# Output projection by output block, gates behind each block, router by input channel block, and the query projected second

## The reference, cut to what matters

```python
# attention of layer 0, per batch: y is what the recurrence gave
q, k, v = x @ Wq.T * K ** -0.5, x @ Wk.T, x @ Wv.T
g = log_sigmoid(x @ Wg.T)
...
o = layernorm(y, gamma, beta) @ Wo.T
x = x + o
# condition of the expert layer, ratio = num / den of the two-sided sum
h = sigmoid(x) * (num / den) * (0.8 + 0.2 * tf)
# router and shared expert
scores = sigmoid(h @ gate_weight.T)          # 16 experts, top 6 of them are picked
shared = down(silu(gate(h)) * up(h))         # 704 inner channels, of every token
```

## Time and profile before

| | us |
|---|---|
| three executions | 3680.26, 3672.75, 3676.23; median 3676.23 |
| the profiled execution, own time | 3678.08 |
| its span, first to last instruction | 3676.3 |
| TensorE clock granted, mean over the span | 0.948 of full |
| busy: PE / DVE / ACT / POOL | 3287.4 / 2605.3 / 1227.3 / 511.8 |

### The profile page before, as it was taken

The page is one execution under the profiler, slowest core; times in us unless marked ns, Lnnn a source line. Parts: engine busy times, 40 slices in busy tenths (PEclk is TensorE's granted clock), DMA queues, the critical chain, the costliest instruction groups (busy, mean ns, idle before and its releaser), DMA issues.

```text
span 3676.3 us, 37190 instructions
## 1 busy us (share of the span) xinstructions
PE 3287.4 (89%) x12621; PEld 2021.7 (55%) x12621; DVE 2605.3 (71%) x3645; ACT 1227.3 (33%) x2145; POOL 511.8 (14%) x404
## 2 busy tenths in 40 slices
PE   1979979979988999999999949899989999999999
PEld 1654654644645767777777714644464446444644
DVE  7888988889875677888888435664667456755664
ACT  2333343332422545434343223312341134113410
POOL 1003003003003111111111021120121012100200
PEclk9989989989999999999999978999999989999999
DMA  3212212212204778787878540223022311222011
GB/s 147 79 34 57 77 45 68 55 48 59 68 15 168 266 248 272 241 276 253 270 245 268 174 189 35 80 94 118 34 81 72 122 53 54 95 91 86 17 53 46
DMA packets 277070, 436.70 MB, mean 119 GB/s; under 512 B 52368, under 2 KB 189584, under 8 KB 264464
## 3 DMA queue, kind: packets, MB, share of 16 engines
q1 hardware_dynamic: 257200, 379.85, 30.9%
q0 software_dynamic: 19680, 54.46, 4.7%
HBM read 364.59 MB, written 93.77 MB: 125 GB/s over the span
## 4 chain that ended last, share of the span: by engine, by line
PE 62%; DVE 23%; DVEq 5%; ACT 5%; issue 2%; DMA 2%; POOL 1%; SPq 0%; ACTq 0%; POOLq 0%
PE bank L1029 13%; PE bank L1058 7%; PE bank L1302 6%; PE bank L1316 4%; PE bank L1324 4%; PE bank L1168 3%; PE bank L838 3%; PE bank L1229 3%; DVE sb_gla L1920 3%; PE bank L978 3%; PE bank L1035 2%; DVE sb_ratio L1878 1%; DVE sb_parts L1932 1%; DVE sb_ratio L1899 1%; PE bank L1024 1%
## 5 line engine op out<-in xcount | busy, mean ns | idle before, releaser
L1029 PE MATMUL bank<-sb_xT,sb_work 128*128 128x256 f32 x2304 | 513.2, 382 | 1.6 <-issue 0.8
L1029 PEld LDWEIGHTS bank<-sb_xT,sb_work 128*128 128x128 f32 x2304 | 439.3, 192 | 75.3 <-issue 17.5
L838 PE MATMUL bank<-sb_gla,sb_work 128*128 128x256 f32 x896 | 244.5, 423 | 64.7 <-DVE sb_work L1922 56.2
L1058 PE MATMUL bank<-sb_work,sb_hT 128*128 128x512 f32 (+1 forms) x666 | 296.1, 592 | 0.0
L838 PEld LDWEIGHTS bank<-sb_gla,sb_work 128*128 128x128 f32 x896 | 179.9, 208 | 123.5 <-DVE sb_work L1922 79.0
L1316 PE MATMUL bank<-sb_parts,sb_gla 128*128 128x512 f32 x512 | 238.5, 610 | 4.5 <-ACT sb_gla L1658 4.5
L1324 PE MATMUL bank<-sb_parts,sb_gla 128*128 128x512 f32 x512 | 230.8, 593 | 6.6 <-DVE sb_work L2510 6.6
L1168 PE MATMUL bank<-sb_parts,sb_hT 128*128 128x512 f32 x512 | 235.7, 621 | 0.0
L1716 POOL DMA_INDIRECT sb_parts<-scratch_h,sb_small x111 | 121.1, 1091 | 820.9 <-DMA sb_small<-scratch_ids 806.3
L1302 PE MATMUL bank<-sb_work,sb_parts 128*128 128x512 f32 (+2 forms) x640 | 227.5, 514 | 5.5 <-ACT sb_work L1671 5.5
L1058 PEld LDWEIGHTS bank<-sb_work,sb_hT 128*128 128x128 f32 (+1 forms) x666 | 121.8, 190 | 129.7 <-issue 129.6
(11 more groups left out here) (397 smaller groups left out, 5919.9 us busy)
## 6 DMA issues: line engine op xcount, KB each, us to landing
sb_work<-scratch_gu SPq DMA_DIRECT2D x63, 1408.0 KB, 7.1
sb_parts<-scratch_mx SPq DMA_DIRECT2D x16, 3072.0 KB, 11.3
sb_work<-moe_w SPq DMA_DIRECT2D x63, 512.0 KB, 6.6
scratch_y<-sb_work SPq DMA_DIRECT2D x48, 512.0 KB, 7.4
sb_parts<-scratch_fq SPq DMA_DIRECT2D x24, 1024.0 KB, 8.6
sb_work<-w_qkvg SPq DMA_DIRECT2D x64, 256.0 KB, 3.2
scratch_gu<-moe_w SPq DMA_DIRECT2D x32, 512.0 KB, 6.1
sb_parts<-fT SPq DMA_DIRECT2D x48, 256.0 KB, 5.7
```

Source lines behind the costliest of these rows:

```text
L838: mm = pe.matmul(dst.rearrange("p (h n l) -> p h n l", h=HPC, l=size), kS[u % 2][:, k * P:(k + 1) * P], late[:, :, k, :, 1, :], start=True ...
L1029: mm = pe.matmul(dst, egu[j % 3][:, which * NC + k, m * P:(m + 1) * P], xt[j % 2][:, k, :], start=(k == 0), stop=(k == NC - 1))
L1058: mm = pe.matmul(bank(YB[s]), einter[j % 2][0:n, a:a + P], edn[j % 3][0:n, m * D:(m + 1) * D], start=(m == 0), stop=(m == EC - 1))
```

## The change

- The output projection has the output block outside and the input block inside, with banks `OB = (7, 1, 2, 3)`; the sum of the squares (L944) comes after the first output block. The waits for the four centred blocks are all in the first output block.
- On DVE the gate of a block follows the sum of the next block (`gate1`), and each gate sets a semaphore of its own. `h1` moves off `yT`: it lies in `ysq` for the first three batches and in `R[0]` for the last.
- The logits have the channel block outside and the token tile inside, and wait for one gate at a time; the 16 small products in one bank are one accumulation.
- Pieces 24 and 25 go from before the sums to behind the gates. Pieces 26 to 28 go from behind the gates into the shared expert: the first tile has `picks` first and then 26 and 27 (before: 29, then `picks`), the second tile has 28 to 33 (before: 30 to 33).
- `PIECES = (3, 0, 1, 2)`: the query is projected second and the key third. POOL waits for two evacuations before `qa` and for the third before `qk`.

```diff
-        h1_ready, m_mask, m_slot = series("row_dve", 3)
+        *h1_ready, m_mask, m_slot = series("row_dve", NC + 2)
...
-        PIECES = (3, 1, 0, 2)
-        OB = (1, 2, 3, 7)
+        PIECES = (3, 0, 1, 2)
+        OB = (7, 1, 2, 3)
         yT = w(8192, NC * T)
-        h1 = yT
         ysq = w(10240, NC * T)
+        H1 = [ysq] * (NB - 1) + [R[0]]
...
-        SHARED_PIECES = (range(29, 30), range(30, 34), range(34, 36), range(36, 40), range(40, 44), range(44, 48))
+        SHARED_PIECES = (range(26, 28), range(28, 34), range(34, 36), range(36, 40), range(40, 44), range(44, 48))
...
-                for k in range(NC):
-                    pe.wait_ge(ln_cent.sem, ln_cent.at(b, k + 1))
-                    for oc in range(NC):
+                for oc in range(NC):
+                    for k in range(NC):
+                        if oc == 0:
+                            pe.wait_ge(ln_cent.sem, ln_cent.at(b, k + 1))
                         mm = pe.matmul(bank(OB[oc]), wo[:, k, oc * P:(oc + 1) * P], ch(yT, k),
                                        start=(k == 0), stop=(k == NC - 1))
-                        if k == NC - 1:
-                            mm.then_inc(o_done.sem, 1)
-                    if k == 0:
+                    mm.then_inc(o_done.sem, 1)
+                    if oc == 0:
...
-                pe.wait_ge(h1_ready.sem, h1_ready.at(b, 1))
-                for t in range(NT):
-                    for k in range(NC):
+                h1 = H1[b]
+                for k in range(NC):
+                    pe.wait_ge(h1_ready[k].sem, h1_ready[k].at(b, 1))
+                    for t in range(NT):
                         mm = pe.matmul(bank(7)[:, t * NE:(t + 1) * NE], ch(h1, k)[:, t * P:(t + 1) * P],
-                                       gwT[:, k * NE:(k + 1) * NE], start=(k == 0), stop=(k == NC - 1))
+                                       gwT[:, k * NE:(k + 1) * NE], start=(k == 0 and t == 0),
+                                       stop=(k == NC - 1 and t == NT - 1))
...
-                    act.activation(ch(h1, c), ch(X1[b % 2], c), ACT.Sigmoid).then_inc(sig1.sem, 1)
+                    act.activation(ch(H1[b], c), ch(X1[b % 2], c), ACT.Sigmoid).then_inc(sig1.sem, 1)
...
-                    pool.wait_ge(g_evac.sem, g_evac.at(u, 3))
+                    pool.wait_ge(g_evac.sem, g_evac.at(u, 2))
                     if u:
                         pool.wait_ge(g_qe.sem, g_qe.at(u - 1, 1))
                     pool.tensor_tensor(qa, qS[u % 2], aS[u % 2], ALU.mult).then_inc(g_pool.sem, 1)
+                    pool.wait_ge(g_evac.sem, g_evac.at(u, 3))
...
-                if b + 1 < NB:
-                    for n in (24, 25):
-                        ratio_piece(r0 + n)
+                def gate1(c):
+                    dve.wait_ge(sig1.sem, sig1.at(b, c + 1))
+                    tt(ch(H1[b], c), ch(H1[b], c), ch(R[1], c), ALU.mult).then_inc(h1_ready[c].sem, 1)
+
                 x = X1[b % 2]
                 for oc in range(NC):
...
                     stt(out=ch(x, oc), in0=ch(ysq, oc), scalar=wob[:, oc:oc + 1], in1=ch(x, oc),
                         op0=ALU.add, op1=ALU.add).then_inc(x1a.sem, 1)
-                dve.drain()
-                for c in range(NC):
-                    dve.wait_ge(sig1.sem, sig1.at(b, c + 1))
-                    q = tt(ch(h1, c), ch(h1, c), ch(R[1], c), ALU.mult)
-                q.then_inc(h1_ready.sem, 1)
+                    if oc:
+                        gate1(oc - 1)
+                gate1(NC - 1)
+                dve.drain()
                 if b + 1 < NB:
-                    for n in (26, 27, 28):
+                    for n in (24, 25):
                         ratio_piece(r0 + n)
...
                     if j == 0:
+                        picks(b)
                         if not last:
-                            ratio_piece(6 * (2 * NC * b + NC) + SHARED_PIECES[0][0])
-                        picks(b)
+                            for n in SHARED_PIECES[0]:
+                                ratio_piece(6 * (2 * NC * b + NC) + n)
```

## The result

The changed kernel took **3644.97 us** (median of 4 runs, 3639.18 to 3650.05) against 3674.49 (4 runs) for the kernel before: ratio 0.9919, 95% interval 0.9907 to 0.9931, so 29.8 us less (25 to 34). I had forecast 3656 and a range of 3649 to 3666.

The account below looks back on a forecast made before the run. The prediction took DVE to set the pace in the first three batches and a dependent chain in the last; 16.2 + 7.3 - 3.4 = 20.1 us off the profiled 3678.08 gave 3658.0, as a median 3656, range 3649 to 3666.

Parts of the forecast that it names:

- What bounds: First three batches: DVE sets the pace, only its own idle time can be had; the last batch has no such cap.
- Sums, gates, logits: End of attention, second batch: last gate at 529.3, DVE's pieces end at 534.4, routing starts there, 7.7 us earlier.
- 16.2 us for three batches: Projection through shared expert, first three batches: DVE's waits for PE go, 16.2 us gained in all.
- gain 5.4 for each of three batches: Each of the first three batches: 6.3 us of waits go; 0.7 in the sums and some 0.2 of semaphores come.
- The last batch, 7.3: Last batch: logits end 8.0 us earlier, less 0.7 for a later clock fall; gain 7.3, bounds 4.2 and 8.9.
- the middle of 1063.3 and 1066.3: Last batch's logits: end at 1063.3 at full clock, 1066.3 at half; the prediction took 1064.2 as the middle.
- Going through the twelve units ... -3.4: Query second: POOL's earlier `qa` meets a ratio piece in seven of twelve units, 4.3 us lost less 0.9 saved.
- the old place: POOL's `qa` before the change: beside a predicated copy, said to cost 0.2 us at one unit of a batch.
- my own slower rival: Attention units: `qa` costs its whole 1.27 us and PE's longer waits let the clock fall; 3692 us, chance 0.06.
- The next batch does not start earlier: Between batches: something beside DVE sets the start, so only the last batch counts; about 3672 us, chance 0.08.
- The sum: Whole kernel: 16.2 + 7.3 - 3.4 = 20.1 us gained.

## Why the prediction was right or wrong

- **What bounds.** Right. DVE's work and idle time set the first three batches, and 92.4 us of work stayed as it was.
- **Sums, gates, logits.** Right to 0.1 us at the steps compared in the profiled second batch (+13.4, +18.5, one wait of 0.6). The clock went a middle way, as taken: in the second batch the first half of the logits ran at full clock and the second in 2.67 us.
- **16.2 us for three batches** came out as 12.4 in the mean of four traces. From the profiled pair alone it is 5.3, 4.9 and 4.6, so 14.9. The step "gain 5.4 for each of three batches" took its before value from one trace with 107.3 in every batch, and in three others four of nine stretches were 105.3 to 105.5; the change had 103.2 and 103.6 in two of its twelve.
- **The last batch, 7.3:** 6.9 to the last sums, less 0.5 to the first expert tile. That its logits end where forecast is in part luck: the middle of 1063.3 and 1066.3 is 1064.8 and not 1064.2, so the term should have been 6.7 and the end 16.0 us behind L938, where 15.0 to 16.0 were measured.
- **"Going through the twelve units ... -3.4"** is the step that failed. It took every collision of `qa` with a ratio piece as lost time, 4.3 us, and priced the old place by what DVE lost there, 0.2 us at one unit of a batch. The collisions came, 3.9 us, and cost nothing that shows; the old place was the dear one, because PE stood behind that instruction at the end of a wait: +6 us by the kernel before with the query second, two measurements, 4.4 of them in the four second units. That a longer wait for DVE costs the clock stood in my own slower rival; I used it against the change alone, not for the instruction that the change takes away.
- **"The next batch does not start earlier"** (0.08) did not come: the batch does start earlier, and the load ahead of it is issued earlier with it. A delay of up to 4.0 us in the second batch's first unit stands in the traces' means, behind `fT` and at a lower clock; whether the change causes it is open. The row against this rival, no DVE wait over 0.2 us between batches, was from the third batch and says nothing of the second.
- **The sum.** 12.4 + 6.4 + 6 is 24.8, and 20.8 if the 4.0 are the change's; the traces' means say 24.4, of which 3.4 is the experts' scatter, and three measurements 22 to 30. The direction and the size of the other terms were right, if the first is 3.8 too high; the range missed the first measurement because the query's term was 9 us too low and because a median of four runs of this kernel moves by several us (28 runs of before on one chip: 3656 to 3681). The errors partly cancel: 3.8 too much and 9 too little.

Not settled: how many us the `fT` wait would give, why the load takes 15 to 21 us from issue in different traces, and whether a part of the query's 6 us lies outside the second units.

## What to carry to other kernels

Add up the busy time and the idle time of the engine that sets the pace over a stretch: if the busy part stays, a change is worth the idle time it removes less what it uncovers, and work that is moved away may have been covering another wait. Where TensorE waits for a Vector instruction, price a delay of that instruction by what TensorE runs at behind the wait, not by its own length. And take several traces of a kernel whose runs scatter by 20 us before reading a difference of a few.

## What was not expected of the hardware

- A small difference in a wait goes with a large one in the clock: behind PE's wait of 0.97 us 25 of 32 sets of scores took over 2.5 us instead of 1.99, behind 0.72 to 0.81 us 2 of 40, and these two stood behind 0.79 and 0.81. In the unit shown that was held 1.07 us, the wait of 1.94 had both next sets at 3.78, and that of 0.86 both at 1.99.
- Behind a hole of 3.09 us the 32 rows of logits took 5.7 us in three batches and 6.98 in one; behind one of 7.4, or of 5.9 in the last batch, they took 7.01 in all sixteen batches of the four traces of before. Behind a wait of 0.52 the second 16 rows of the changed kernel took from 1.96, full clock, in four batches of sixteen, to 3.46.
